# Attention of batches 2 and 3, expert 0's weights and the first gathered chunk moved to earlier places

## The reference

```python
x = x + layernorm(attn(layernorm(x)))      # x is 4 x 2048 x 256
x = x + layernorm(ffn(layernorm(x)))
# attn: 16 heads of 16 features; the softmax runs over a head's 16x16 matrix of features
qk, v  = x @ Wqk, x @ Wv
logits = (2*dot(qk,qk) - q2[...,:,None] - q2[...,None,:]) / sqrt(N) * tau
out    = concat_heads(softmax(logits) @ v) @ Wo
# ffn: one shared expert for all 8192 tokens, and 7 routed ones, the best 2 of 7 per token
h      = layernorm(x) * ln_g + ln_b
top_vals, top_idx = top_k(h @ Wr, 2);  gates = softmax(top_vals)
# each expert takes its first 732 tokens by position in a running count; others are dropped
y      = (silu(xe @ W1) * (xe @ W3)) @ W2   # 256 -> 1024 -> 256, the shared expert alike
out    = routed + shared
```

## Time and profile before

| | |
|---|---|
| median of 3 runs | 1161.42 us (1160.91 to 1162.58) |
| profiled execution | 1161.56 us |
| its span on the core | 1159.8 us |
| PE busy | 1077.1 us, 93% |
| DVE, ACT, POOL busy | 675.8, 514.8, 377.3 us |
| mean granted clock of PE | 0.974 |

### The profile page before, as it was taken

How to read it: one execution, slowest core, us unless ns; L and a number is a source line. 1 busy time by engine, 2 the same in 40 slices (tenths; PEclk the granted TensorE clock), 3 DMA queues, 4 the chain that set the end, 5 groups by cost and what they waited for, 6 DMA issues and landing times. The chain is left out here.

```text
span 1159.8 us, 19315 instructions
## 1 busy us (share of the span) xinstructions
PE 1077.1 (93%) x6744; PEld 984.6 (85%) x6744; DVE 675.8 (58%) x1727; ACT 514.8 (44%) x911; POOL 377.3 (33%) x333
## 2 busy tenths in 40 slices
PE   4579999999999999999999988999999999999980
PEld 3468788898888898888898877999999999999870
DVE  6466784467764467764468522635455463545796
ACT  2333344344434344444345323546445454554664
POOL 3420643011550011650012562433443343222223
PEclk9889999999999999999999998999999999999995
DMA  8852341114421114422114434425253242246596
GB/s 302 287 166 92 115 136 62 37 55 160 151 80 68 37 56 145 164 67 80 37 56 170 152 105 137 120 54 138 46 125 93 70 128 45 68 110 181 189 340 235
DMA packets 83275, 140.89 MB, mean 121 GB/s; under 512 B 10356, under 2 KB 60664, under 8 KB 83200
## 3 DMA queue, kind: packets, MB, share of 16 engines
q1 hardware_dynamic: 66864, 112.45, 29.2%
q0 software_dynamic: 16336, 27.48, 9.4%
HBM read 73.19 MB, written 66.69 MB: 121 GB/s over the span
## 5 line engine op out<-in xcount | busy, mean ns | idle before, releaser
L1549 DVE TENSOR_TENSOR sb_act<-bank,sb_act 128x512 f32<-128x512 f32 (+2 forms) x240 | 148.7, 619 | 368.9 <-PE bank L1056 341.9
L1054 PE MATMUL bank<-sb_h_hi,sb_wup_lo 128*128 128x512 f32 (+2 forms) x960 | 354.8, 370 | 8.4 <-DVE sb_h_lo L1519 6.1
L1056 PE MATMUL bank<-sb_h_hi,sb_wup_hi 128*128 128x512 f32 (+2 forms) x960 | 351.2, 366 | 0.0
L1055 PE MATMUL bank<-sb_h_lo,sb_wup_hi 128*128 128x512 f32 (+2 forms) x960 | 350.8, 365 | 0.0
L984 ACT ACTIVATE sb_act<-bank 128x512 f32<-128x512 f32 (+2 forms) x240 | 129.9, 541 | 425.8 <-PE bank L1056 368.6
L1054 PE MATMUL bank<-sb_wdn_hi,sb_act_lo 128*128 128x256 f32 (+1 forms) x848 | 247.9, 292 | 3.9 <-DVE sb_act_lo L1525 3.3
L1056 PE MATMUL bank<-sb_wdn_hi,sb_act_hi 128*128 128x256 f32 (+1 forms) x848 | 238.8, 282 | 0.0
L1055 PE MATMUL bank<-sb_wdn_lo,sb_act_hi 128*128 128x256 f32 (+1 forms) x848 | 238.3, 281 | 0.0
L1054 PEld LDWEIGHTS bank<-sb_h_hi,sb_wup_lo 128*128 128x128 f32 x960 | 181.7, 189 | 26.8 <-DVE sb_h_lo L1519 6.7
L1056 PEld LDWEIGHTS bank<-sb_h_hi,sb_wup_hi 128*128 128x128 f32 x960 | 181.4, 189 | 22.9
L1055 PEld LDWEIGHTS bank<-sb_h_lo,sb_wup_hi 128*128 128x128 f32 x960 | 182.1, 190 | 17.8
(11 more groups left out here) (192 smaller groups left out, 1314.6 us busy)
## 6 DMA issues: line engine op xcount, KB each, us to landing
sb_xin<-in_L_ffn_W_dram SPq DMA_DIRECT2D x28, 512.0 KB, 4.4
sent_scratch<-sb_early SPq DMA_DIRECT2D x8, 1548.0 KB, 8.4
sb_x<-in_L_attn_x_dram SPq DMA_DIRECT2D x16, 512.0 KB, 4.7
x_scratch<-sb_x SPq DMA_DIRECT2D x16, 512.0 KB, 3.8
sb_xin<-in_L_attn_x_dram SPq DMA_DIRECT2D x14, 512.0 KB, 5.6
y_scratch<-sb_ysb SPq DMA_DIRECT2D x14, 512.0 KB, 4.0
sb_xn<-in_L_ffn_W_dram SPq DMA_DIRECT2D x14, 512.0 KB, 4.7
hT_scratch<-sb_hr SPq DMA_DIRECT2D x12, 512.0 KB, 2.7
```

The source lines that it names most:

```text
L1054: t_.matmul(o, a_lo, b_hi, start=start, stop=False, skip_group_check=True)
L1055: t_.matmul(o, a_hi, b_lo, start=False, stop=False, skip_group_check=True)
L1056: return t_.matmul(o, a_hi, b_hi, start=False, stop=stop, skip_group_check=True)
L1549: v.tensor_tensor(act[:, m % 2, 0:c.w], bank[(4 if c.wide and m % 2 else 0) + 1][:, 0:c.w], act[:, m % 2, 0:c.w], ALU.mult).then_inc(act_o ...
```

## The change

The places of some steps are lower numbers now:

- The X steps of batch 3 begin at place 131 (before 136). Batch 2's stay at 72.
- The M steps of batches 2 and 3 take 10 places, with batch 1's spacing, from 93 and 152 (before 92 and 156, over 17 places).
- The O steps begin at 105 and 164 (before 110 and 174); routing and sends move with them. In the last batch the count and what follows it for the second pair stand at 31, 33, 33, 34 places behind the first O step, before 31, 33, 34, 34.
- Expert 0's weight pieces are steps of the schedule: loads at place 153 (pieces 0 to 2) and 187, 189, 191; high parts at 182 to 192, low parts at 184 to 194, at even places; `indices` at 200.

Sends of a group wait until the group two before it has landed. Spare rows are now different for the groups of a pair and lie behind the old end of the scratch, which is longer by 2048 rows. Chunk 12 is wide too: it uses two pairs of PSUM banks in turn for its ups, as chunk 13 did. The first gathered chunk is the next of chunk 13: its turns stand at m = 4 and 5 of chunk 13, its preps there and at m = 6. Chunk 13's last downs and its take_y stand inside expert 0's first part.

```diff
-            cs = [shared_chunk(n // GB, n % GB, n == FIRST - 1) for n in range(FIRST)]
-            return list(zip([None] + cs[:-1], cs, cs[1:] + [None]))
+            cs = [shared_chunk(n // GB, n % GB, n >= FIRST - 2) for n in range(FIRST)]
+            return list(zip([None] + cs[:-1], cs, cs[1:] + [expert_chunk(0, 0, 1)]))
...
-            body(None, expert_chunk(0, 0, 1), expert_chunk(0, 1, 1))
+            body(shared_chunk(B - 1, GB - HELD - 1, True), expert_chunk(0, 0, 1), expert_chunk(0, 1, 1))
...
+        M_FIRST_AT = (20, 22, 23, 24, 25, 26, 27, 28, 30, 31, 32, 33, 34, 35, 36, 36, 37)
+        M_AT_PLACES = (0, 1, 1, 2, 2, 3, 3, 4, 5, 5, 6, 7, 8, 8, 9, 9, 10)
...
+        X_AT, MIX_AT = (None, 14, 72, 131), (None, 46, 105, 164)
         for b in range(1, B):
-            origin = PLACES * (b - 1)
-            put(b, origin, 0, [("x_first", 0)])
-            origin += LEAD
+            put(b, X_AT[b] - 8 if b > 1 else 0, 0, [("x_first", 0)])
             for q in range(GB):
-                put(b, origin + 4 * q + (6 if b == 1 else 0), q, X_STEPS + X_LOWS)
+                put(b, X_AT[b] + 4 * q, q, X_STEPS + X_LOWS)
+            put(b, MIX_AT[b] - 12, 0, zip(M_STEPS, M_AT_PLACES))
             for q in range(GB):
-                put(b, origin + 38 + 5 * q, q, O_STEPS)
+                put(b, MIX_AT[b] + 5 * q, q, O_STEPS)
...
+        for j in range(PIECES):
+            put(B - 1, 0, j, [("w_next", 153 if j < 3 else 181 + 2 * j), ("w_high", 182 + 2 * j), ("w_low", 184 + 2 * j)])
+        put(B - 1, 0, 0, [("indices", 200)])
...
+            def w_next(b, j):
+                if j == 0:
+                    for k in range(4):
+                        sp.wait_ge((xn_ok, xlo_ok, xt_ps, xt_ps)[k], OPEN + NG * (1, 1, 2, 2)[k])
+                        sp.sem_inc(sp_go, 1)
+                load_piece(1, j, [W1[0], W3[0]], W2[0], stage_later)
...
-            made(v.iota(lostid[:, :, :], [[0, 2], [P, GT * 2]], base=2 * E * ROOM, channel_multiplier=1,
+            made(v.iota(lostid[:, :, :], [[GT * 2 * P, 2], [P, GT * 2]], base=SENT_ROWS, channel_multiplier=1,
...
-                        elif q > 0:
-                            pool.wait_ge(sent[q - 1], b * SENT + SENT)
+                        if q > 1:
+                            pool.wait_ge(sent[q - 2], b * SENT + SENT)
                         else:
-                            pool.wait_ge(sent[GB - 1], b * SENT)
+                            pool.wait_ge(sent[q + 2], b * SENT)
...
-            high(cs[-1][1], FM - 1)
-            take_y(cs[-1][1])
-            for k in range(KC):
-                prep(expert_chunk(0, 0, 1), k)
...
-            for m in (FM - 2, FM - 1):
-                down(cs[-1][1], m)
-            for k in range(KC):
-                turn(expert_chunk(0, 0, 1), k)
...
-            low(cs[-1][1], FM - 1)
-            prep(expert_chunk(0, 0, 1))
```

More of the change, by code:

```diff
@@ L74, in sandwich_kernel @@
     SENT_ROWS = 32 * SPARE * P
-    assert LASTW < P and 2 * E * ROOM + 2 * GT * P <= SENT_ROWS
+    assert LASTW < P and 2 * E * ROOM <= SENT_ROWS
     assert D == KC * P and ST == 6 and E == 7 and GB == 4 and FM == 8
@@ L394, in sandwich_kernel @@
         PLACES = 2 * FM * GB
-        LEAD = 8
-        BEFORE = PLACES - LEAD
-        LAST = 2 * FM * (FIRST - GB + HELD)
+        BEFORE = 56
         END = 2 * FM * FIRST
@@ L427, in sandwich_kernel @@
         put(0, -BEFORE, 2, [("x_low0", 8 + 6)])
-        put(0, -BEFORE, 0, M_STEPS_AT)
+        put(0, -BEFORE, 0, zip(M_STEPS, M_FIRST_AT))
         put(0, -BEFORE, 2, [("x_low1", 24)])
@@ L478, in attend @@
                     steps[name](b, q)
-        INDEX_AT = 17
         CLEARS = 32 // CLEAR
@@ L610, in shared_places @@
                 for place in range(2 * FM):
-                    if place == (5 if n == 0 else 2) and j < GB - 1:
+                    if place == (5 if n == 0 else 2) and j < GB - 1 and n + 1 < FIRST:
                         load_h(b, j + 1)
@@ L615, in shared_places @@
                     attend(steps, 2 * FM * n + place)
-            for n in range(FIRST - HELD):
+            for n in range(FIRST):
                 shared_places(n)
-            b = B - 1
-            for k in range(4):
-                sp.wait_ge((xn_ok, xlo_ok, xt_ps, xt_ps)[k], OPEN + NG * (1, 1, 2, 2)[k])
-                sp.sem_inc(sp_go, 1)
-            for j in range(3):
-                load_piece(1, j, [W1[0], W3[0]], W2[0], stage_later)
-            load_h(b, 1)
-            for place in range(LAST, END):
-                if place == LAST + 6:
-                    store_y(b - 1, GB - 1)
-                attend(steps, place)
-            for j in range(3, PIECES):
-                load_piece(1, j, [W1[0], W3[0]], W2[0], stage_later)
-            for j in range(GB - HELD):
-                store_y(b, j)
+            store_y(B - 1, GB - HELD - 1)
             for j in range(NZERO):
@@ L999, in _ @@
                 attend(steps, place)
-            def route(place):
-                if place % 2 and 3 <= place < 3 + 2 * PIECES:
-                    high_piece(1, (place - 3) // 2, 1, stage_later)
-            def between(place):
-                attend(steps, place)
-                if place >= LAST:
-                    route(place - LAST)
-            cs = first_chunks()
-            for prev, c, nxt in cs:
-                body(prev, c, nxt, lambda place: between(2 * FM * c.n + place))
-            high(cs[-1][1], FM - 1)
-            take_y(cs[-1][1])
-            for k in range(KC):
-                prep(expert_chunk(0, 0, 1), k)
+            steps["w_high"] = lambda b, j: high_piece(1, j, 1, stage_later)
+            for prev, c, nxt in first_chunks():
+                body(prev, c, nxt, lambda place: attend(steps, 2 * FM * c.n + place))
             def body_and_weights(prev, c, nxt):
@@ L1569, in _, with indices @@
                 attend(steps, place)
-            def indices():
+            def indices(b, q):
                 ch = Chain(dve, i_chain, 0)
@@ L1582, in indices @@
                 dve.sem_inc(r_idx, 1)
-            def route(place):
-                if place % 2 and 5 <= place < 5 + 2 * PIECES:
-                    j = (place - 5) // 2
-                    if j == 4:
-                        dve.wait_ge(sent[0], B * SENT)
-                    low_piece(1, j, 1, stage_later)
-                if place == INDEX_AT:
-                    indices()
-            def between(place):
-                attend(steps, place)
-                if place >= LAST:
-                    route(place - LAST)
-            cs = first_chunks()
-            for prev, c, nxt in cs:
-                body(prev, c, nxt, lambda place: between(2 * FM * c.n + place))
-            low(cs[-1][1], FM - 1)
-            prep(expert_chunk(0, 0, 1))
+            steps["w_low"] = lambda b, j: low_piece(1, j, 1, stage_later)
+            steps["indices"] = indices
+            for prev, c, nxt in first_chunks():
+                body(prev, c, nxt, lambda place: attend(steps, 2 * FM * c.n + place))
             def body_and_weights(prev, c, nxt):
```

18 lines of the change are left out of this document (7 added, 11 removed).

## The result

The changed kernel takes 1154.49 us (median of 4 runs, 1153.3 to 1155.51), beside 1162.0 of the kernel before: 0.9922 of its time, interval 0.9905 to 0.994. Faster, as forecast, but 7.5 us above the 1147 that I gave and outside the range. The profiled execution took 1154.1 with a span of 1152.4, so it stands for the runs. All of this holds on one kind of chip only: in two later sets the same kernel was 3.1 and 2.6% slower than the kernel before.

The account below looks back on a forecast made before the run. TensorE, busy 93% of the span, was taken as the bound, losing time only when standing still or at low clock. 1161.56 - 11.6 - 3.6 - 0.8 + 1.3 = 1146.9, stated as 1147 us; range 1144.5 to 1152.

Parts of the forecast that it names:

- Handoff: From chunk 13 to the first gathered chunk: preparing the latter inside chunk 13 gains 11.6 us if rows arrive in time.
- Hole in chunk 12: PE's idle time and low clock near 642 us go with expert 0's weights sooner: 3.6 us gained.
- POOL's wait near 142: In batch 1's opening, sends waiting two groups back end a wait that reaches PE: 0.8 us gained.
- The pressed chain: Small products of batches 2 and 3, 17 places pressed into 10: cost 0 per chain, bounds 0 and 10.7 us.
- third rival: Pressed chains of batches 2 and 3 stall PE, making the kernel slower than before: up to 1168 us; chance 0.03.
- Crowding: VectorE, busier at places 182 to 193, is late for PE: 1.3 us lost, bounds 0 and 3.7.
- Slack of the gather: At the handoff, gathered rows land 4 to 5 us before PE wants them at 671 us.
- rival 2: The gather is late and part of the handoff's hole stays: 1152 us, up to 1156 with late weights; chance 0.10.
- The routed part, the held chunks and the tail move as a block: Work after the handoff shifts as a whole, since its waits hang on each other; no change in its time.

Follow-up runs that it names:

- d4: The kernel before with only the first gathered chunk prepared inside chunk 13; attention, weights and sends stay: 1178.74 us, 1.0101 of the kernel before.
- b3: The changed kernel with sends again waiting for the group just before, new spare rows kept: 1163.42 us, 1.000 of the kernel before.
- f3: The changed kernel with the first gathered chunk made ready after chunk 13, as before, on another chip: 1216.26 us, 1.0397 of the kernel before.
- b2: The changed kernel with only batch 2's softmax one place sooner: 1150.42 us, 0.9895 of the kernel before.
- b1: The changed kernel with batch 2's chain of small products one place sooner, from 92: 1149.96 us, 0.9886 of the kernel before.
- h2: The changed kernel with sends two groups back in batch 3 alone, batch 2's chain one place sooner, expert 0's weight pieces spread: 1147.87 us, 0.9878 of the kernel before.
- h1: The changed kernel with sends waiting two groups back in batch 3 alone, one group back elsewhere: 1154.29 us, 0.9931 of the kernel before.
- b0: The changed kernel once more, unaltered, in the first follow-up set: 1154.28 us, 0.9921 of the kernel before.
- f0: The changed kernel once more, unaltered, on the third set's chip: 1205.84 us, 1.0312 of the kernel before.

## Why the prediction was wrong

The sum had 14.7 us of gain, the profiled runs show 7.5. By the prediction's own words it is wrong as a mechanism twice over: the time is above 1152, and the handoff is closed while another hole of over 3 us stands elsewhere, at 365. Its steps:

- **Handoff, 11.6: right.** Measured 11.8. The fused handoff needs the early rows (d4, b3), as the step said, and the early rows need the fusing for the other half (f3).
- **Hole in chunk 12, 3.6: right.** 3.8 in the stretch from 640 to 660 us.
- **POOL's wait near 142, 0.8: right.** The stretch has 1.1 less, b3 gives 0.8 of it back.
- **"The pressed chain is the one that batch 1 already has [...] I take 0 per chain": this step failed.** Batch 2's chain costs 5.0 us, batch 3's 0.7. Two thirds of the shortfall of 7.3 us stand in batch 2's. I compared the spacing of the places and not their parity: batch 1 starts at 34, batch 2 at 93. My third rival had the price range (bounds 0 and 10.7) and its sign, a wait on the small products, came at 365 in one chain. It had density as the cause, which b2 rules out for this wait, and I gave it 0.03, since "PE did not wait" in batch 1. b1 and b2 show the step at 4.3 and 3.9 us.
- **Crowding, 1.3: mis-sized.** 2.6 by h2 beside h1, and 2.5 by the stretch from 600 to 640. PE's own waits in the rows above add up to 1.34, just my number; the distances from start to start show twice that. Such a list leaves out delays too small to be rows of it.
- **Slack of the gather, 4 to 5: mis-sized, at no price.** It was 2.9. PE and the sends both came some 8 us later than I had them (PE asks at 679.00, not at 671; the last pair's sendto is cast at 643.47, not at 636), mostly by the losses before, and that cancels. The slow sends' 4.0 us do not, as I had taken 1.265 for each. Three more as slow as the slowest and rival 2 would have begun. My sentence that the trace has the sends at 0.96 us was read from single rows: in the trace before, 16 of 128 take over 1.25 us, the longest 2.11.
- **"The routed part, the held chunks and the tail move as a block": right within 0.2.** The last stretch loses 1.1 more and the time behind the last matmul is 0.9 shorter. The opening loses 0.6 more, where the low clock falls on other matmuls. The same kernel's runs differ by more there: 43.2 and 44.5 in the first 80 us for the changed kernel and b0.
- **No step of mine was about the chip.** A trace without one late increment can't show what the pauses of POOL were good for: I had them down as pure idle time (2.76 and 5.76 us in the earlier trace rows).

With the failed step mended and the crowding spread, the kernel takes 1147.87 (h2), 14.4 us below the kernel before, where the forecast had 14.7. That is partly luck: h2 has next to no crowding, which the sum counted at 1.3 against it, and it keeps the wait near 142, which the sum counted as a gain of 0.8.

## What to carry to other kernels

Before a chain of small steps is moved along a schedule, look not only at how far apart its steps stand but at what stands between each pair on both engines; one place of shift put a 1.28 us table load and a 1.06 us copy between an exponential and its sum, and cost 3.4 to 5 us, by what the clock did behind it. A wait that looks like idle time in one trace may hold back traffic that another chip doesn't bear: here a wait taken away gave 9 us on one chip and cost 29 on another. Taking it away only where the time is on the critical path (here the last batch) kept the gain on a chip that bears the traffic; on the other kind it was not tried. Time such a kernel on more than one chip.

## What the runs showed of the hardware

- Increments of semaphores by the engines came late on three of five chips while indirect sends were issued back to back (9.4 us in f0, where Silu starts with the increment), and never over 0.02 us late on the other two; why the chips differ stays open, and so does what the increments wait for. An undisturbed send took 0.96 us on both kinds, and the sends' packets 0.12 us on average.
- A send beside VectorE's tensor_tensor of 1024 columns with both inputs in SBUF took 1.51 to 2.05 us in place of 0.96 (four of four in batch 3 of the changed kernel).
- One table load for the activation is 1.28 us, and the next ACTIVATE starts 0.02 us behind it (361.54, 362.84).
- The same wait of PE of 2.1 us was followed by 3 us at the low clock in the changed kernel and b0 (granted clock 0.96 from 340 to 380 us), and by none in b3 and h1 (1.00); what decides it is open. Waits of 0.75 and 0.79 us were not followed by any.
